# A recurrent last stage rebuilt around tiled matmuls, with its second token shift on GpSimd

## The reference

```python
xa = _ln(x, ln1_w, ln1_b)
sx = concatenate([state[:, 1:2] - xa[:, :1], xa[:, :-1] - xa[:, 1:]], axis=1)      # first token shift
xxx = tanh((xa + sx * maa_x) @ maa_w1).reshape(b, l, 5, DM) ; xxx = einsum('blfd,fde->blfe', xxx, maa_w2)
xk, xw, xv, xr, xg = xa + sx * (maa_stack + xxx)                                    # five mixed inputs
w = exp(-exp(time_decay + tanh(xw @ td_w1) @ td_w2)) ; r, k, v = xr @ Wr.T, xk @ Wk.T, xv @ Wv.T
g = silu(xg @ Wg.T)
def step(s, rkvw):                      # per head: a state of 8 x 8 values
    a = k_t[..., :, None] * v_t[..., None, :]
    out = einsum('bhi,bhij->bhj', r_t, u * a + s)
    s = a + w_t[..., :, None] * s
og = (og - mean) / sqrt(var + 1e-05) * gn_w + gn_b                                  # over the 8 values of a head
x1 = x + og * g @ Wo.T
xc = _ln(x1, ln2_w, ln2_b)
sx2 = concatenate([state[:, 0:1] - xc[:, :1], xc[:, :-1] - xc[:, 1:]], axis=1)      # second token shift
xk2, xr2 = xc + sx2 * ffn_maa_k, xc + sx2 * ffn_maa_r
return x1 + sigmoid(xr2 @ Wfr.T) * (square(relu(xk2 @ Wfk.T)) @ Wfv.T)
```

## Time and profile before

| | us |
|---|---|
| median of 3 runs | 2364.75 (2362.14 to 2367.24) |
| the profiled execution, its own time | 2361.19 |
| its span | 2359.5 |
| of that, the recurrence (from 1883 us to the end) | 476.5 |
| one slot in the middle of it | about 54.6 |

### The profile page before, as it was taken

The page is one execution under the profiler, slowest core; times in us unless marked ns, Lnnn a source line. Parts: engine busy times, 40 slices in busy tenths (PEclk is TensorE's granted clock), DMA queues, the critical chain, the costliest instruction groups (busy, mean ns, idle before and its releaser), DMA issues. The chain is left out here.

```text
span 2359.5 us, 40465 instructions
## 1 busy us (share of the span) xinstructions
PE 2116.9 (90%) x15416; PEld 1857.7 (79%) x15416; DVE 1376.1 (58%) x2740; ACT 955.2 (40%) x2642; POOL 558.5 (24%) x358
## 2 busy tenths in 40 slices
PE   6987886989999999997999999999798788888886
PEld 4665665978999999986899999998797656667775
DVE  6886884345455456454555454654234767877885
ACT  4774776544333333323332333333353222333332
POOL 3553553532000000002200000000352233333331
PEclk9998997999999999998999999999899877878887
DMA  4001003000000000031000000001000000000000
GB/s 153 2 2 37 15 6 134 11 7 6 6 0 4 4 4 4 4 101 50 5 6 0 4 4 4 4 25 58 25 1 19 22 1 1 5 5 4 4 10 9
DMA packets 34357, 45.37 MB, mean 19 GB/s; under 512 B 2145, under 2 KB 26305, under 8 KB 33985
## 3 DMA queue, kind: packets, MB, share of 16 engines
q1 hardware_dynamic: 34240, 43.78, 5.5%
HBM read 33.28 MB, written 2.10 MB: 15 GB/s over the span
## 5 line engine op out<-in xcount | busy, mean ns | idle before, releaser
L693 ACT ACTIVATE arena<-banks 128x512 f32<-128x512 f32 x128 | 72.9, 596 | 417.0 <-PE banks L574 414.2
L686 ACT ACTIVATE arena<-banks,arena 128x129 f32<-128x129 f32 x512 | 180.7, 375 | 135.3 <-DVE arena L737 135.3
L501 POOL TENSOR_TENSOR w_hT_lo<-arena,w_hT_hi 128x512 fp32r<-128x512 f32 x16 | 21.2, 1324 | 901.8 <-ACT w_hT_hi L661 901.8
L362 DVE TENSOR_TENSOR x_new<-x,banks 128x512 f32<-128x512 f32 x32 | 22.0, 688 | 364.6 <-PE banks L606 234.6
L606 PE MATMUL banks<-arena 128*128 128x256 f32 x1024 | 229.6, 382 | 0.0
L606 PEld LDWEIGHTS banks<-arena 128*128 128x128 f32 x1024 | 191.9, 190 | 35.4 <-issue 10.6
L756 DVE COPY arena<-banks 128x512 f32<-128x512 f32 x128 | 88.6, 692 | 210.3 <-PE banks L584 210.3
L928 POOL TENSOR_TENSOR arena<-arena 128x1024 f32<-128x1024 f32 x64 | 150.2, 2371 | 136.8 <-DVE arena L1187 136.8
L1121 ACT ACTIVATE arena<-arena 128x128 f32<-128x128 f32 x512 | 162.5, 394 | 3.5 <-DVE arena L1196 3.3
L116 PE MATMUL banks<-w_hT_lo,w_hi 128*128 128x256 f32 x512 | 151.8, 296 | 6.8 <-POOL w_hT_lo L501 6.8
L116 PE MATMUL banks<-w_kv_lo,w_hi 128*128 128x256 f32 x512 | 145.2, 284 | 3.8 <-DVE arena L723 3.8
(11 more groups left out here) (275 smaller groups left out, 5759.3 us busy)
## 6 DMA issues: line engine op xcount, KB each, us to landing
arena<-ctx_t SPq DMA_DIRECT2D x32, 256.0 KB, 2.5
arena<-in_L_xattn_wq SPq DMA_DIRECT2D x8, 512.0 KB, 4.2
arena<-in_L_xattn_wk SPq DMA_DIRECT2D x8, 512.0 KB, 5.6
arena<-in_L_xattn_wv SPq DMA_DIRECT2D x8, 512.0 KB, 6.8
arena<-in_L_xattn_wo SPq DMA_DIRECT2D x2, 2048.0 KB, 13.0
x<-in_x SPq DMA_DIRECT2D x4, 512.0 KB, 5.5
arena<-in_L_xattn_w SPq DMA_DIRECT2D x2, 1024.0 KB, 11.2
ctx_t<-in_ctx_t SPq DMA_DIRECT2D x1, 2048.0 KB, 12.5
```

The source lines that it names most:

```text
L686: done = act.activation(prob[:, b, i, :], score_tile(c, j), ACT.Exp, scale=SCALE, bias=shift[:, b, i:i + 1], accum_out=total[:, b, i:i + 1])
```

## The change

Only the recurrence and the layout of its inputs change.

1. **Units.** `spread_v` handles both sequences of a feature half at once: 8 matmuls with 32 rows and 256 columns, four row groups of the array into four banks, twice a slot in place of four times. The value features are reordered on the host (`by_value`), so the four row groups hold different values. `u * kv` leaves the unit. In its place a "bonus" is computed per pair: r times k on GpSimd (`multiply_rk`), one matmul pair with `bonus_w`, one product with v on VectorE (`make_bonus`). The product with r moves from GpSimd to VectorE, straight on the states. `kv` gets two buffers, and ScalarE writes its first column.
2. **Head sums.** `head_sum` is now the stationary operand (32 columns) and the product moves; four column groups of the array. The result has features on the partitions.
3. **Group norm** becomes two TensorE steps (`centre` with identity minus mean, `variance` with the mean matrix), a square, a logarithm and an exponential on ScalarE, one product on VectorE, scale and bias on ScalarE (`scale_rows`), and the gate on GpSimd. The transposes before `Wo` go.
4. **`shift_c` on GpSimd**: one subtraction, then for `xk2` and for `xr2` two `tensor_scalar` of 256 columns and one addition of 512.
5. k, v and the gate move: copies of k and v to ScalarE, the g projection into the `a` part, the final addition (`finish`) to GpSimd, straight into `x`. The slots are written out, with no loop, from -1 to 8.

```diff
-                for j in range(J):
-                    mm = pe.matmul(VB[:, j, :], pick[:, j, :], vT[:, par, k, b * P:(b + 1) * P], start=True, stop=True)
+                for j in range(JJ):
+                    for a in range(NT):
+                        rows = slice(a * ROWS_OF, (a + 1) * ROWS_OF)
+                        mm = pe.matmul(bank[a][:, j * PT:(j + 1) * PT], pick[rows, j, :], vT[rows, parity(p), k, :], start=True, stop=True)
...
-                for j in range(J):
-                    at = (b * KC + k) * P + j * HT
-                    mm = pe.matmul(OG[:, at:at + HT], prod[:, s % 2, j, :], head_sum[:, :], start=True, stop=True)
+                for j in range(JJ):
+                    for a in range(NT):
+                        mm = pe.matmul(OG[a * ROWS_OF:(a + 1) * ROWS_OF, s * P:(s + 1) * P], head_sum[:, j, :, :].rearrange("p e h -> p (e h)"),
+                                       prod[:, n % 2, a * JJ + j, :], start=(j == 0), stop=(j == JJ - 1))
...
+            def bonus_sums(a):
+                pe.wait_ge(rk_ok, a + 1)
+                pe.wait_ge(read["rate"], a + 1)
+                wait(pe, read["rr"], a - 1)
+                for k in range(KC):
+                    mm = pe.matmul(X[:, k * PT:(k + 1) * PT], bonus_w[:, k, :], rk[:, k, :], start=True, stop=True)
+            def centre(p):
+                pe.wait_ge(raw_ok, p + 1)
+                pe.wait_ge(read["c"], p + 1)
+                pe.matmul(OG[:, :], centre_w[:, :], raw[:, :], start=True, stop=False)
+                pe.matmul(OG[:, :], centre_w[:, :], bonus[:, parity(p), :, :].rearrange("p k t -> p (k t)"), start=False, stop=True).then_inc(centred, 1)
+            def variance(p):
+                pe.wait_ge(square_ok, p + 1)
...
+                pe.matmul(Y[:, :], mean_w[:, :], square[:, :], start=True, stop=True).then_inc(ready["var"], 1)
...
+            def shift_c(c):
+                gp.wait_ge(read["xc"], c + 1)
+                gp.wait_ge(c_first, c + 1)
...
+                gp.tensor_tensor(sx2[:, :, :, :].rearrange("p k b t -> p (k b) t"), xc[:, :, :, 0:P].rearrange("p k b t -> p (k b) t"),
+                                  xc[:, :, :, 1:P + 1].rearrange("p k b t -> p (k b) t"), ALU.subtract).then_inc(shift2_ok, 1)
...
+                for i, (to, n) in enumerate(((xk2, "ffn_maa_k"), (xr2, "ffn_maa_r"))):
+                    for k in range(KC):
+                        gp.tensor_scalar(to[:, k, :], flat(sx2[:, :, :, :])[:, k, :], core.col(pre + n, k), None, ALU.mult).then_inc(scaled_ok, 1)
+                    gp.wait_ge(scaled_ok, (c * 2 + i + 1) * KC)
...
+                    gp.tensor_tensor(rows, rows, xc[:, :, :, 1:P + 1], ALU.add).then_inc(xk_ok, 1)
...
+            def square_centred(p):
...
+                act.activation(square[:, :], OG[:, :], ACT.Square).then_inc(square_ok, 1)
+            def group_rstd(p):
...
+                act.activation(log_var[:, :], Y[:, :], ACT.Ln, bias=core.eps[:, 0:1]).then_inc(read["var"], 1)
...
+                act.activation(grstd[:, :], log_var[:, :], ACT.Exp, scale=-0.5).then_inc(grstd_ok, 1)
...
+                dve.tensor_tensor(prod[:, n % 2, :, :], states[:, :, 0:P],
+                                  rT[:, parity(p), k, tokens(b)][:, None, :].to_broadcast([P, J, P]), ALU.mult).then_inc(prod_ok, 1)
...
+            def unit_variance(c):
+                dve.wait_ge(grstd_ok, c + 1)
```

More of the change, by code:

```diff
@@ L2069, in slot @@
                 if u:
[L2070 removed]
+                    make_decay(p, 3)
                 if c:
[L2072 to L2076 removed]
+                    row_rstd(p - 1)
@@ L2089, in slot @@
[L2089 to L2102 removed]
+                    make_decay(p + 1, 1)
```

669 lines of the change are left out of this document (362 added, 307 removed).

## The result

The changed kernel takes 2298.6 us (median of 4, 2296.9 to 2302.9) against 2364.6 (2362.1 to 2367.2) for the kernel before: a ratio of 0.9724, 95% interval 0.9705 to 0.9742, or 66 us less. The forecast was 2304.0.

The account below looks back on a forecast made before the run. No engine fills the slot; a chain through engines taking turns bounds it. First unit 1918 + slot 0 34 + six slots of 46 + end 71 = span 2299, giving 2304 us (range 2281 to 2321).

Parts of the forecast that it names:

- 11.2 us of TensorE's work: Spreads and head sums in a slot: 15.6 us before, 4.4 in the new forms.
- P: Interval between the first units of successive pairs, one middle slot: 55.0 us before, predicted 46.
- gone from the path of each unit: Recurrence units: GpSimd's turn for the product with r, 2.35 us, no longer stands in each unit's path.
- The 72.3 us of waits in three slots: Kernel before: GpSimd waits twelve times for VectorE's L2163, read as showing where engines take turns.
- The walk through the slot: One changed slot followed engine by engine from VectorE's unit 0: 42.0 us at the full clock.
- The clock: TensorE groups behind two idle stretches (3.1 and 3.8 us) run at the lower clock: 4 us of a possible 10.
- the rival of a cold second half: TensorE at the lower clock for each slot's second half: slot 49 to 53 us, 2322 to 2346; chance 0.20.
- the slower one: Idle stretches keep TensorE at the lower clock nearly throughout: slot 58 us, time 2376; chance 0.04.
- GpSimd's `tensor_scalar`: Second shift's scaling of 256 columns on GpSimd: 0.41 us each, interpolated, four of them.
- the upper bound: GpSimd instruction starting inside a VectorE scan waits for the rest of it, up to 2.31 us, not 0.37.
- The rival of a GpSimd hardly held: GpSimd hardly waits for VectorE, or TensorE keeps full clock: slot 38 to 42 us, 2256 to 2280; chance 0.18.
- the rival of groups in series: Row and column groups don't run side by side: head sums 1.7, spread 3.5, slot 53 us, 2346; chance 0.04.

Follow-up runs that it names:

- Run 11: Kernel before with six of the eight matmuls of each spread and each head sum left out: 2318.7 us.
- run 9: Changed kernel with head sums issued four times and spreads three times, product with r left on VectorE: 2338.4 us.
- run 4: Changed kernel with the product of states with r back on GpSimd and two buffers of states: 2306.7 us.
- run 7: Changed kernel with head sums issued four times, spreads three times and the product with r back on GpSimd: 2351.4 us.
- run 12: Kernel before with a quarter of the spread and head-sum matmuls, and four of VectorE's seven group norm instructions left out: 2311.2 us.
- run 1: Changed kernel with the second token shift put back on VectorE: 2280.6 us.
- run 8: Changed kernel with second shift on VectorE, dummy matmuls around unit 0's head sums, first mixes before unit 1's head sums and spread after the third mix: 2251.1 us.
- run 3: Changed kernel with the matmuls of each unit's head sums issued four times: 2311.4 us.
- run 2: Changed kernel with six and two unused dummy matmuls in TensorE's idle stretches before and behind unit 0's head sums: 2290.5 us.
- run 5: Changed kernel with second shift on VectorE and dummy matmuls around unit 0's head sums, both at once: 2264.4 us.

## Why the prediction was right, and where it was not

**What bounded it.** The prediction said that no engine did, that TensorE's spreads and sums and the turns of each unit were the slot, and that 11.2 us of TensorE's work would go. Run 11 shows 6.8 of the 10.5 us of P from that alone, run 9 shows 4.8 from the other side. The other named gain, the turn on GpSimd at 2.35 us a unit "gone from the path of each unit", is much smaller: 0.8 a slot in run 4, 2.0 on top of the heavier TensorE (run 7 against run 9). The 72.3 us of waits in three slots can't have been its cost: they were for the most part time in which GpSimd had nothing else to do. Taking work off VectorE on top of run 11 gave nothing in P (run 12). Which of the remaining edits gives the last 3.7 us between run 11 and the changed kernel stays open. It is 5.5 us against run 1, as the second shift on GpSimd takes 1.8 back.

**The sum came out by compensation.** Against the span of 2299 the first unit is 6.8 late, slot 0 1.2 short, six slots 9.2 short together and the tail 5.8 long, which makes + 2.2. The late first unit is not the change: VectorE's first normalisation starts 9.7 us later than before (1894.1 against 1884.4), in stages whose code is the same. In the profiled executions of the other runs it starts between 1886.7 and 1895.4, so this is scatter between executions. From there to the first unit it is 30.7 us against 28.7, so the prologue grew by 2 where 5 was predicted. GpSimd's constants fitted, as claimed. That the span came out within 2.2 us is luck: a late start and a long tail stood against shorter slots.

**The walk through the slot**, in us after unit 0's start:

| | predicted | measured |
|---|---|---|
| `unit_variance` ends | 6.2 | 6.4 |
| unit 1 ends | 13.15 | 13.4 |
| `a_low` ends | 10.3 | 12.3 |
| mixes end | 20.0 | 21.7 |
| xc ready | 23.8 | 27.3 |
| `xk2` ready | 29.7 | 34.2 |
| unit 3's product ends | 33.6 | 33.2 |
| `xr2` ready, `Wfr` starts | 35.3 | 37.3 |
| next slot | 42.0 (+ 4 for the clock) | 44.4 |

The group norm's chain is right to 0.2 us, and so is unit 1. VectorE's work was forecast at 31 us and is 32.6. Its old shift was read too low: four at some 0.45 us each, where the slot of before has 3.63 for the four together. TensorE's work was forecast at 28 for the full clock; run 8 has 35.7 at clock 1.00, of which the dummies are 2.83 + 1.13 = 4.0, so 31.8. The mixes were the largest piece missing, 1.14 + 1.91 = 3.1 us where 2.0 was written; the eight projections take 14.6 from start to start in run 8's slot where 13.8 was written, and the rest is in small pieces. Three terms were off, these 3.8 us of TensorE's work and two more:

- *The clock* (4 us: "one group at each stretch with its neighbour, 1.0 and 3.0"). It cost 1.6. `a_low` and `Wo` lost (3.92 - 2.11) + (2.92 - 1.99) = 2.7 us, then td and k (1.97 and 2.70 against 1.08 and 1.99 in run 3) 1.6 more, a place that I hadn't named. That is 4.3 us of longer groups, near the 4 of the forecast, but 1.04 of it is covered by unit 1 and the part in td and k by the slow shift: four slots of run 2 are 42.8 us, among them the one with `a_low`, `Wo`, td and k all at the full clock. So the walk's 42.0 stands against 42.8, and the clock's 4 against 44.4 - 42.8 = 1.6. The predicted 3.8 us of idle before `Wfr` was split in two, 0.80 and 1.07, since `Wfk` came later; the clock stayed at 1.00 there, and nothing of the 3.0 was lost. This also fells the rival of a cold second half, and the slower one.
- *GpSimd's `tensor_scalar`* (0.41 predicted, 0.92 measured). The shift without rivals is 7.3 us, not 5.5, as the last slot shows:

```profile
2283.15 1.04 POOL L1841 TENSOR_TENSOR arena<-arena 128x512 f32<-128x512 f32 x1 [10.31 <-ACT arena L2184]
2284.29 1.83 POOL L1847 TENSOR_SCALAR arena<-arena,cols 128x256 f32<-128x256 f32 x2
2286.20 1.18 POOL L1850 TENSOR_TENSOR arena<-arena 128x512 f32<-128x512 f32 x1
2287.36 1.83 POOL L1847 TENSOR_SCALAR arena<-arena,cols 128x256 f32<-128x256 f32 x2
2289.26 1.18 POOL L1850 TENSOR_TENSOR arena<-arena 128x512 f32<-128x512 f32 x1
```

  1.8 us of the tail's 5.8 are this. GpSimd was busy 19.35 us in the slot where 15 was forecast; the price of the four `tensor_scalar` is 2.0 us of that, and most of the rest is holding (1.5 in the first pair, 0.7 in the subtraction, 0.4 in the addition behind).

**Holding.** I took the upper bound, the rest of a whole VectorE instruction, against the 0.37 us that a row showed. That was right: L1847 went to 2.46 us when it started inside a scan, 1.54 more than undisturbed, where the row had 0.37. The rival of a GpSimd hardly held is out. Less of it fell in the slot than the walk had, 2.6 us (9.9 - 7.3) where it had 5.9 (11.4 - 5.5), since `xc` came 3.5 us later and met the end of unit 2.

**The price of the titled step.** The prediction gave shift costs (3.3 us to `xk2`, 5.5 to `xr2`, 2.6 on VectorE) but no time for a kernel with the shift left on VectorE. Run 1 gives it: 14 to 18 us, 1.8 in each of six slots and 6.9 in the tail.

**Rows and columns in groups.** Head sums at 0.64 (0.55 predicted) and spreads at 1.15 (1.1): the rival of groups in series is out.

## What to carry to other kernels

Price a step from both sides, by a run that takes it out of the old kernel and one that puts it back into the new: here single edits gave 8 and 13 us, and both with the spreads gave 53. When two chains end within a few tenths of a microsecond of each other (0.37 in run 11), shorten both or neither. Before moving work to an idle engine, look at how long its instructions are and what they share: 2.4 us on VectorE became 7.3 to 9.9 on GpSimd, in the chain to the last projections, while a few dummy matmuls in TensorE's waits and one reordering gave 30 us (run 1 to run 8). And look at every slot of a run, not at one: the same program had slots of 38.8 and 40.4 us (run 5).
